# Attention in double steps: shift groups of two pairs, and every fourth pair scored once with queries on partitions

## The reference, cut to what matters

```python
q = jnp.einsum('bnd,hde->bhne', query, Wq) * scale
k = jnp.einsum('bmd,hde->bhme', query, Wk)
v = jnp.einsum('bmd,hde->bhme', query, Wv)
logits = jnp.einsum('bhne,bhme->bhnm', q, k)
attn = jax.nn.softmax(logits, axis=-1)
out = jnp.einsum('bhnm,bhme->bnhe', attn, v)
out = jnp.swapaxes(out, -1, -2).reshape(B, N, E * H)
return jnp.dot(out, Wp) + bp
...
x = x + _L0_attn_ref(_layernorm(x, axis=-1), ...)
x = x + _L0_ffn_ref(_layernorm(x, axis=-1), ...)
```

## Time and profile before

| what | us |
|---|---|
| median of 3 runs | 992.97 (990.68 to 994.6) |
| the profiled execution's own time | 992.29 |
| span of the profile | 990.5 |
| TensorE busy | 968.2 (98%) |
| GpSimd busy | 861.8 (87%) |
| VectorE busy | 854.4 (86%) |
| ScalarE busy | 733.4 (74%) |

### The profile page before, as it was taken

One profiled execution on the slowest core, in us unless ns is written; L12 is line 12 of the kernel. 1 busy time (PEld: TensorE's weight loads), 2 busy tenths in 40 slices (PEclk: granted clock), 3 DMA queues, 4 the chain that ended last, 5 costly groups with the idle time before them and its releaser, 6 DMA issues.

```text
span 990.5 us, 39211 instructions
## 1 busy us (share of the span) xinstructions
PE 968.2 (98%) x15932; PEld 767.8 (78%) x15932; DVE 854.4 (86%) x1743; ACT 733.4 (74%) x1180; POOL 861.8 (87%) x849
## 2 busy tenths in 40 slices
PE   7899999999999999999999999999999999989998
PEld 6577777787787887777778878877888887767776
DVE  6898988888888898899888988898888988768787
ACT  4687777778777777777777777777777778677775
POOL 5789898989886999999999999999899999878885
PEclk9999999999999999999999999999999999999999
DMA  6112232342323333223333332233433333367885
GB/s 136 44 31 53 47 74 53 62 64 64 79 43 51 64 84 65 61 51 59 85 63 64 58 83 39 61 61 83 65 63 64 63 64 63 79 126 158 168 171 129
DMA packets 242786, 74.08 MB, mean 75 GB/s; under 512 B 218032, under 2 KB 240304, under 8 KB 242608
## 3 DMA queue, kind: packets, MB, share of 16 engines
q1 hardware_dynamic: 240528, 71.05, 36.7%
q10 hardware_dynamic: 2080, 0.52, 0.3%
HBM read 11.41 MB, written 8.39 MB: 20 GB/s over the span
## 4 chain that ended last, share of the span: by engine, by line
PE 92%; DVE 2%; ACT 2%; issue 1%; DMA 1%; POOL 1%; SPq 0%; DVEq 0%; ACTq 0%; POOLq 0%
PE S L765 11%; PE PV L790 8%; PE M L725 7%; PE PV L792 6%; PE PV L791 6%; PE QK L712 5%; PE QK L714 5%; PE QK L713 5%; PE misc L765 5%; PE S L757 5%; PE M L843 2%; PE M L808 2%; PE M L845 2%; PE M L844 2%; PE misc L757 2%; PE M L810 2%
## 5 line engine op out<-in xcount | busy, mean ns | idle before, releaser
L1325 POOL TENSOR_TENSOR pl<-p 128x1024 f16<-128x1024 f32 x253 | 476.6, 1896 | 33.1 <-ACT p L1102 32.8
L1526 DVE TENSOR_REDUCE negmax<-M 128x4 f32<-128x1024 f32 x252 | 306.7, 1217 | 22.2 <-PE M L725 16.2
L1110 ACT ACTIVATE QKh<-QK 128x512 f16<-128x512 f32 x251 | 149.5, 596 | 142.2 <-PE QK L714 141.4
L1102 ACT ACTIVATE p<-S,s_exp 128x1024 f32<-128x1024 f32 x173 | 192.2, 1111 | 56.9 <-PE S L765 56.3
L790 PEld LDWEIGHTS PV<-V,p 128*128 128x128 bf16 x2048 | 186.6, 98 | 47.1 <-issue 36.3
L790 PE MATMUL PV<-V,p 128*128 128x65 f16 x2048 | 214.8, 193 | 4.5 <-DVE O L1540 3.6
L791 PE MATMUL PV<-V,p 128*128 128x64 f16 x2048 | 213.2, 192 | 0.0
L792 PE MATMUL PV<-V,pl 128*128 128x65 f16 x2048 | 212.5, 194 | 0.0
L1546 DVE TENSOR_TENSOR QKl<-QK,QKh 128x512 f16<-128x512 f32 x251 | 172.3, 687 | 43.3 <-ACT QKh L1110 42.2
L791 PEld LDWEIGHTS PV<-V,p 128*128 128x128 bf16 x2048 | 189.0, 97 | 4.7
L792 PEld LDWEIGHTS PV<-V,pl 128*128 128x128 f16 x2048 | 188.7, 97 | 0.0
(11 more groups left out here) (246 smaller groups left out, 2472.4 us busy)
## 6 DMA issues: line engine op xcount, KB each, us to landing
y_kept<-yTb SPq DMA_DIRECT2D x32, 128.0 KB, 1.7
yT<-y_kept SPq DMA_DIRECT2D x16, 256.0 KB, 3.4
result<-X SPq DMA_DIRECT2D x15, 256.0 KB, 3.0
X<-in_L_attn_query SPq DMA_DIRECT2D x7, 512.0 KB, 4.2
OT<-O SPq DMA_TRANSPOSE x64, 4.1
shift<-negmax SPq DMA_TRANSPOSE x63, 2.3
O<-in_L_attn_Wk ACTq DMA_DIRECT2D x2, 256.0 KB, 4.8
O<-in_L_attn_Wq SPq DMA_DIRECT2D x2, 256.0 KB, 5.6
```

The lines of the kernel that those rows point to most:

```text
L1102: e.activation(p32[r][:, :, :, :].rearrange("p i m n -> p (i m n)"), score_bank(p)[:, :], ACT.Exp, scale=s_exp[:, :]).then_inc(s_ex, 1)
L1325: e.tensor_tensor(pl[r][:, :, :, :].rearrange("p i m n -> p (i m n)"), p32[r][:, :, :, :].rearrange("p i m n -> p (i m n)"), p_high(r).rea ...
L1526: e.tensor_reduce(dst[:, :, NB * jj:NB * jj + NB], max_bank(p)[:, :].rearrange("p (i t m) -> p i t m", i=2, t=NB), AX.X, ALU.max, negate=T ...
```

## The change

- Shift groups hold two pairs instead of four, and pairs are prepared less far ahead: Q and K by 5 instead of 7, maxima by 4 instead of 6. Of the start-up, max_scores(3), max_scores(4) and queries_keys(4) move behind scores(0), and the maxima of Wp and g2 go to step 9.
- Double steps begin at 56 instead of 80. In them weighted and normalise handle t-3 and t-2 instead of t-2 and t-1.
- Each p with p % 4 == 3 from 75 to 235, 41 pairs, is **direct**. Each is the odd pair of a D-step. It has no max_scores and no shift. `direct_scores` makes its exact scores once, queries on partitions, in `misc`, as the first work of the D-step; `direct_max` (VectorE) takes the maxima there, ScalarE scales them to a bias (128 x 4) and takes the exponential in four calls of 256 columns, each with its own column of the bias; `direct_high` (ScalarE) and `direct_low` (GpSimd) write the two parts to `p_rows`, and a transfer (`turn_p`) of 128 x 2048 values turns them for `weighted`, two double steps later.
- Some preparation of the feed-forward weights moves by a few steps (`second_weights` in the double steps), and the last steps pair their score banks from NP - 4 instead of NP - 6.

```diff
-GP = 4
+GP = 2
...
-Q_LEAD, MAX_LEAD, PV_LAG = 7, 6, 3
+Q_LEAD, MAX_LEAD, PV_LAG = 5, 4, 3
...
-PAIRED = NP - 6
-TWO_0, TWO_1 = 80, 240
-LOW_ON_DVE = (NP - 5, NP - 3, NP - 1)
...
-MAXIMA = {"pg": (None, 7, 8), "t1": (45, 46, 54)}
+PAIRED = NP - 4
+TWO_0, TWO_1 = 56, 240
+DIRECT_0, DIRECT_1 = 75, 238
+LOW_ON_DVE = (NP - 3, NP - 1)
...
-    first = {0: [5, 6], 1: [7, 8], 2: [9], TWO_1: []}
+    first = {0: [4, 5], TWO_1: []}
     return first.get(t, [t + Q_LEAD] if t + Q_LEAD < NP else [])
...
+def direct(p):
+    return p % 4 == 3 and DIRECT_0 <= p < DIRECT_1
+def direct_no(p):
+    return sum(direct(k) for k in range(p))
+def maxima_to(p):
+    return p + 1 - direct_no(p + 1)
+def exps_to(p):
+    return p if direct(p) else p + 2 if direct(p + 1) else p + 1
 def weighted_pair(t):
-    return t - PV_LAG if 0 <= t - PV_LAG < NP and t != TWO_1 else None
+    return t - PV_LAG if 0 <= t - PV_LAG < NP else None
 def max_pairs(t):
-    first = {0: ([], [5]), 1: ([6], [7])}
+    first = {1: ([4], [5])}
+    if t == 0:
+        return [3], []
     return first.get(t, ([t + MAX_LEAD] if t + MAX_LEAD < NP else [], []))
...
-        a = [sb(f"a{i}", [P, F]) for i in range(A_RING)]
+        a_all = sb("a_all", [P, A_RING, F])
+        a = [a_all[:, i, :] for i in range(A_RING)]
+        p_rows = a_all[:, 2:4, :].rearrange("p a f -> p (a f)").bitcast(F16).rearrange("p (s c) -> p s c", s=2)
+        p_turned = a_all[:, 0:2, :].rearrange("p a f -> p (a f)").bitcast(F16)
+        neg_rows, bias_rows = sb("neg_rows", [P, 2, NB]), sb("bias_rows", [P, 2, NB])
         zTh = [sb(f"zTh{i}", [P, FC, P], BF16) for i in range(3)]
...
+            def turn_p(p):
+                d = direct_no(p)
+                e.wait_ge(s_dhi, d + 1)
+                e.wait_ge(s_dlo, d + 1)
+                if d:
+                    e.wait_ge(s_pv, p - 3)
+                e.dma_start_transpose(p_turned.rearrange("p (c n) -> p c n", n=P),
+                                      p_rows.rearrange("p s c -> p (s c)")).then_inc(p_in_turned, 16)
             def turn_y(b):
...
+                    if t and direct(t - 1):
+                        turn_p(t - 1)
+                    if t == 0:
+                        turn_x(1)
                     if x_split_batch(*divmod(t - 1, HP)) is not None:
...
                 elif jj == 0:
-                    e.wait_ge(shift_in, 16 * g)
+                    e.wait_ge(shift_in[g % 2], shift_turned(g))
...
                 elif TWO_0 + 1 < p < TWO_1:
-                    e.wait_ge(s_ex, p - 1)
+                    e.wait_ge(s_ex, exps_to(p - 2))
                 elif p == PAIRED:
-                    e.wait_ge(s_mx, NP)
+                    e.wait_ge(s_mx, maxima_to(NP - 1))
                 elif p > PAIRED:
...
                                 op.then_inc(s_sc, 1)
+            def direct_scores(p):
+                h, lo = QKh[p % QK_RING], QKl[p % QK_RING]
+                e.wait_ge(s_qklo, p + 1)
+                e.wait_ge(s_ex, exps_to(p - 2))
+                for t in range(NB):
+                    tok = slice(t * P, (t + 1) * P)
+                    for n, (q, k) in enumerate(((h, h), (lo, h), (h, lo))):
+                        for i in range(2):
+                            rows = head_rows(i)
+                            op = e.matmul(misc_pair[:, i * 512 + t * N:i * 512 + (t + 1) * N], q[rows, 0, tok], k[rows, 1, :],
+                                          start=n == 0, stop=n == 2, skip_group_check=True)
+                            if t == NB - 1 and n == 2:
+                                op.then_inc(s_sc, 1)
+            def p_parts(p, i, m, t):
+                if direct(p):
+                    parts = p_turned.rearrange("p (s i t m n) -> p s i t m n", s=2, i=2, t=NB, m=NB)
+                    return parts[:, 0, i, t, m, :].bitcast(BF16), parts[:, 1, i, t, m, :]
...
+                tok = slice(t * P, (t + 1) * P)
+                return p_high(p % P_RING)[:, i, m, tok], pl[p % P_RING][:, i, m, tok]
             def weighted(p):
                 b, j = divmod(p, HP)
-                r = p % P_RING
...
                 op.then_inc(s_yp0 if t == 0 else s_yp, 1)
             def two_steps(t):
+                if direct(t + 1):
+                    direct_scores(t + 1)
                 if t > TWO_0:
                     e.wait_ge(*two_free(t - 2))
+                    if t - 2 in PREPARED:
+                        e.wait_ge(s_w, W_AT[PREPARED[t - 2]])
                 max_scores(t + MAX_LEAD)
                 scores(t)
-                scores(t + 1)
-                max_scores(t + 1 + MAX_LEAD)
-                weighted(t - 2)
+                if not direct(t + 1):
+                    scores(t + 1)
+                if not direct(t + 1 + MAX_LEAD):
+                    max_scores(t + 1 + MAX_LEAD)
+                weighted(t - 3)
                 queries_keys(t + Q_LEAD + 1)
                 for piece in two_values(t):
                     values(*piece)
                 if two_project(t):
                     project_tile(*two_project(t), t)
-                weighted(t - 1)
+                second_weights(t)
+                weighted(t - 2)
                 queries_keys(t + Q_LEAD + 2)
...
                 e.activation(shift[0][:, :], misc("shift", 0)[:, 0:P], ACT.Copy, scale=1.0 / SHIFT_UP).then_inc(s_sh16, 1)
             def shift_rounded(g):
-                e.wait_ge(s_mx, GP * g + GP)
...
                              scale=s_exp[:, :]).then_inc(s_ex, 1)
+            def direct_exps(p):
+                r, d = p % P_RING, direct_no(p)
+                e.wait_ge(s_dmx, d + 1)
+                e.activation(bias_rows[:, :, :], neg_rows[:, :, :], ACT.Identity, scale=s_exp[:, :]).then_inc(s_dbias, 1)
+                e.wait_ge(s_dbias, d + 1)
+                if d:
+                    e.wait_ge(s_dlo, d)
+                else:
+                    e.wait_ge(s_pv, p - P_RING + 1)
+                for i in range(2):
+                    for t in range(NB):
+                        op = e.activation(p32[r][:, i, t, :], misc_pair[:, i * 512 + t * N:i * 512 + (t + 1) * N], ACT.Exp,
+                                          scale=s_exp[:, :], bias=bias_rows[:, i, t:t + 1])
+                op.then_inc(s_ex, 1)
+            def direct_high(p):
+                d = direct_no(p)
+                e.wait_ge(s_ex, exps_to(p))
+                if d:
+                    e.wait_ge(p_in_turned, 16 * d)
+                e.activation(p_rows[:, 0, :].bitcast(BF16), p_high(p % P_RING).rearrange("p i m n -> p (i m n)"),
+                             ACT.Copy).then_inc(s_dhi, 1)
             def qk_high(p):
...
                 b, j = divmod(t, HP)
                 if shift_group(t) is not None:
                     shift_rounded(shift_group(t))
-                exps(t)
-                exps(t + 1)
+                if direct(t + 1):
+                    direct_exps(t + 1)
+                    exps(t)
+                    direct_high(t + 1)
+                else:
+                    exps(t)
+                    exps(t + 1)
                 qk_high(t + Q_LEAD + 1)
                 for piece in two_values(t):
                     v_high(*piece)
...
+            def direct_low(p):
+                r, d = p % P_RING, direct_no(p)
+                e.wait_ge(s_ex, exps_to(p))
+                if d:
+                    e.wait_ge(p_in_turned, 16 * d)
+                e.tensor_tensor(p_rows[:, 1, :], p32[r][:, :, :, :].rearrange("p i m n -> p (i m n)"),
+                                p_high(r).rearrange("p i m n -> p (i m n)"), ALU.subtract).then_inc(s_dlo, 1)
...
                 b, j = divmod(t, HP)
+                if direct(t + 1):
+                    direct_low(t + 1)
                 p_low(t)
                 if x_stats_batch(b, j) is not None:
                     norm_root(x_stats_batch(b, j))
-                p_low(t + 1)
+                if not direct(t + 1):
+                    p_low(t + 1)
                 for group in split_groups(b, j):
                     o_low(*group)
                 if j == 4 and b + 2 < B:
...
+            def direct_max(p):
+                d = direct_no(p)
+                e.wait_ge(s_sc, 2 * exps_to(p))
+                if d:
+                    e.wait_ge(s_dbias, d)
+                e.tensor_reduce(neg_rows[:, :, :], misc_pair[:, :].rearrange("p (i t m) -> p i t m", i=2, t=NB),
+                                AX.X, ALU.max, negate=True).then_inc(s_dmx, 1)
...
                 max_out(t + MAX_LEAD)
                 qk_low(t + MAX_LEAD + 1)
-                max_out(t + MAX_LEAD + 1)
-                sums_inverse(t - 2)
-                normalise(t - 2)
+                if not direct(t + 1 + MAX_LEAD):
+                    max_out(t + MAX_LEAD + 1)
+                sums_inverse(t - 3)
+                normalise(t - 3)
                 qk_low(t + Q_LEAD + 1)
                 for piece in two_values(t):
                     v_low(*piece)
                 if two_project(t):
```

(76 more changed lines are left out.)

75 lines of the change are left out of this document (41 added, 34 removed).

## The result

The changed kernel takes **1068.36 us** (median of 3 runs, 1066.66 to 1070.49) where the kernel before takes 992.97: a ratio of 1.0768, with a 95% interval of 1.0748 to 1.0788. It is slower by 75 us, where 66 were forecast.

What follows compares the result with a forecast made beforehand. TensorE, busy 98%, bounds the kernel before; in the changed D-step the order of work would. From 992.3 us, +70 for 41 direct pairs and -3 at the start gave 1059, range 1018 to 1094.

Steps and rivals of the forecast that it cites:

- The chain on ScalarE: D-step: direct work and exps(t) delay qk_high and the second Q and K; +1.7 us a direct pair, +70 us.
- That stall of 1.3 us lies within the longer one: D-step: first Q and K wait 1.3 us for VectorE; hidden within ScalarE's longer stall, so not added.
- The rival priced at 1022 for VectorE's chain alone: D-step: only VectorE's chain holds, the step ends at 7.3 us, +0.8 us a pair, 1022 us; chance 0.07.
- The end: Last pairs: two maxima and two Q/K are less far ahead; 0 us, bounds -2 and +2.
- exps(t+1) now waits for weighted(t-3) of the same step: V-step: this new wait was set against a 0.2 us wait that goes; the step was taken at 6.54 us.
- The start: First steps: reductions, qk_low and the maximum of Wp leave VectorE's path; -3 us, bounds -5 and +2.
- The saving: TensorE: a direct pair drops max_scores and shift, 0.44 us each, 18 us; rival that it comes through: 971 us, chance 0.11.
- The rival's condition: D-step: faster if ScalarE's share between bias and qk_high is under about 2.0 us, taken as 4.2; that rival's chance 0.11.
- The turned p: Transfer for a direct pair's weighted: lands by 16.2 us, needed at 16.6, so it costs nothing.
- the sentence on lost cover: Turned p's transfer: if the D-step's wait on ScalarE no longer covered it, each us of lateness would cost 41 us.
- 1 us for each pair: Rival: the turned p lands late and holds weighted and all behind it on TensorE; 1100 us, chance 0.05.

Runs made afterwards that it cites:

- e3: Changed kernel with direct_high moved behind the second qk_high of a D-step, nothing else; 1032.48 us beside 993.74 for the kernel before.
- e4: Changed kernel with qk_high moved right behind the four exponentials, ahead of exps(t) and direct_high; 1030.26 us beside 993.74 for the kernel before.
- e1: Changed kernel with Y_TURN and Y_KEEP (SyncE's steps for the feed-forward transpose and following copy) back at 6 and 8; 1060.86 us, one run.
- e6: Changed kernel without direct pairs, with weighted and normalise at t-2 and t-1 again; 996.56 us, one run beside 994.51 for the kernel before.
- e8: e6 with Y_TURN, Y_KEEP at 6, 8; one run 989.27 us beside 994.51; 12 more runs 992.93 beside 991.95, ratio 1.0005.
- e2: Changed kernel without any direct pair, all other edits kept; 1009.65 us (2 runs) beside 993.74 for the kernel before, ratio 1.016.
- e9: e7 with turn_shift ahead of turn_p on SyncE's queue again; 995.26 us, one run beside 992.14 for the kernel before.
- e10: e9 with the next step's shift rounded behind the D-step's first qk_high; 995.13 us (8 runs) beside 992.14 for the kernel before, ratio 1.0026.
- e7: Changed kernel, direct work behind the double step's own, turn_p before turn_shift, Y_LAG 0, Y_TURN and Y_KEEP 6, 8; 1002.62 us beside 994.51.

## Why the prediction was right, and where it was off

**The chain on ScalarE was the cause, with nearly its size.** Counted from the first direct matmul at 501.12, term by term:

| step | predicted | measured |
|---|---|---|
| direct_max ends | 2.09 | 2.13 |
| bias ends | 2.46 | 2.46 |
| one exponential, start to start | 0.47 | (505.42 - 503.61) / 4 = 0.45 |
| first Q and K | 3.89 | 505.03: 3.91 |
| exps(t), its end less the overlap | 5.34 | 506.42: 5.30 |
| direct_high, its length less the overlap | 0.96 | 507.36 - 506.42 = 0.94 |
| qk_high ends | 6.90 | 507.97: 6.85 |
| second Q and K starts | 7.66 | 508.76: 7.64 |
| D-step | 8.35 | 509.52: 8.40 |
| V-step behind it | 6.54 | 516.01 - 509.52 = 6.49 |
| both, against before | +1.7 | +1.71 |

The terms lie within 0.06 us of the trace, with both signs, so that they partly cancel. The unshown price, an exponential of 256 columns, had been bounded between 0.42 and 0.59; it is 0.45. The Trainium skill's rule (ScalarE: Activation LUTs, "What ACT_TABLE_LOAD costs") gave an estimated 0.49; a call by itself is 0.562 long in the groups view (mean of 164), by the rule an estimated 0.585. The trace is a little below it. By the rule's figure the sum would have been 4 us higher (0.09 x 41), by the measured one it is 3 lower (0.02 x 4 x 41) than with the 0.47 taken. direct_high's source, every second 16-bit word, costs nothing extra: 1.07 against 1.06 for a plain one.

**"That stall of 1.3 us lies within the longer one"** is right: from start to start it is 1.31 us (503.72 to 505.03), of which the timeline counts 1.15 as idle, and e3 and e4 uncover it. The rival priced at 1022 for VectorE's chain alone is what e4 makes, 1030: with 7.47 instead of 7.3 for its step, and with the end's loss in it.

**The terms that failed are the prices of the end and of the lag.** "*The end*: ... 0, bounds -2 and +2" was worked out for two maxima and two Q and K only. The constants Y_TURN and Y_KEEP were not priced at all: 5.7 us by e1. The last pairs cost another 1.7; e6 and e8 have this too, without direct pairs. The shorter leads and the later start of paired score banks (`PAIRED`) change together there, and no run takes them apart. That "exps(t+1) now waits for weighted(t-3) of the same step" was seen, and the V-step was taken at 6.54 all the same, and double steps from 56 at 0. e2 and e6 together price this lag at 0.29 us for two steps where there are no direct pairs. Between pairs 56 and 75 that would be an estimated 1.2 to 1.5 us, near the 1.3 of the ledger; but from the 50th to the 75th Q and K the changed kernel takes only 0.4 us longer than e6 (86.56 against 86.17), so the rest of the 1.3 has no place yet. In steps with direct pairs it is covered: the V-step is 6.49 long, and direct_scores needs no `M`. The start was taken at -3 and measured -4.7, near its bound of -5; in the traces of the runs, whose starts are nearly the same, it is between -2.1 (e9) and -4.9 (e2) at pair 50, so this term carries a scatter of a few us. Together, from the predicted 1059.3: -1.7 at the start, +1.3 for what fell elsewhere, +0.1 in the chain, +1.7 and +5.9 at the end make 1066.6, the profiled run's time.

**The rivals.** The saving did not come through. With both handovers of `QK` mended (e10) the rate is still 13.24 and not 13.175 - 0.44; whether an order exists that brings it through is not shown. The rival's condition, ScalarE's share between bias and qk_high under 2.0 us, was short of the truth: e4 meets it (1.9 us) and takes 1030, because VectorE's chain lies beneath, which by the prediction's own 7.3 us would have held the step up too. The turned p was late in only 7 waits of 4.6 us in all in the changed kernel; its transfer landed after a median of 4.8 us, where 4.1 had been taken from the earlier trace rows. In e9 and e10, with short D-steps, that cover is gone and it waits 14.0 and 10.5 us, as the sentence on lost cover said it might, though by far less than "1 us for each pair".

## What to carry to other kernels

A bank that is handed on twice in one step makes a chain through the in-order programs of three engines. Before adding work to one of them, write down what will stand between each matmul and the copy that frees its bank, in microseconds, against the margin the trace shows. Here the second handover had a margin of 0.6 us, and ScalarE had 4.1 us to do between VectorE's maxima and qk_high, 2.1 more than the two exponentials that stood there before, while its busy share looked free at 74%. Price every constant that a diff changes, above all those that move a transfer or an order near the end, where no other work covers them. And set the gain against the room: here 0.44 us saved on an engine at 98% did not pay for a transfer, a copy and five activations on engines at 74 to 87%, not even in the best order found.

## What the hardware showed that I had not expected

- In the changed kernel TensorE started nothing between 951.42 and 955.95, and its granted clock was then 0.71 on average from 955 to 960 us, so for part of them at the lower of its two levels (1.2 against 2.4 GHz). In e6, busy for 1.07 us of the 5 behind the last normalise, it was 0.50, the lower level, all through 884.93 to 889.93. In e1 and e8, where the transpose is early, it stayed at 1.00 in these stretches. TensorE's longer wait is 3.2 of the 6.3 us behind the last pair (4.14 - 0.96); these runs take the wait and the lower clock away together, so how much of the rest is the clock's isn't told apart.
- A transpose's issue takes time on the queue itself: mostly 1.12 us for a shift, and between 1.3 and 3.4 us for the 128 x 2048 of turn_p (the queue's timelines of the changed kernel, e7, e9 and e10 from 480 to 530 us). One more in 13 us was enough for the order on the queue to count (e7 against e9).
- A ScalarE call on 4 columns with a scale from a tile takes 0.30 us, half of what the 256-column exponential takes (0.56).
